# Last layer of a two-layer attention and feed-forward network: rows kept on the chip, weights quantised earlier, row scaling on ScalarE

## The chip, the cores and the metric

The kernel runs on one core of a Trainium2 chip. Its engines are TensorE (matrix products and transposes), VectorE, ScalarE, GpSimd, and SyncE, which issues all the DMAs that are spoken of here. Each runs its own list of instructions in order and waits for the others by semaphores. The metric is the device time of one execution in microseconds (us).

## What is computed

Two layers, each a cross attention and a feed-forward part, on x of 8 batches x 512 rows x 256 columns. The first layer has 16 heads of 64 and experts chosen per batch; the second has 16 heads of 16 and a quantised feed-forward part. Cut to the last layer:

```python
x = x + _L1_xattn_ref(_layernorm(x), ctx_768, ...)        # the second attention
x = x + _L1_ffn_ref(_layernorm(x), W_in, b_in, W_out, b_out)

def _L1_ffn_ref(x, W_in, b_in, W_out, b_out):             # 256 -> 1024 -> 256
    W_in_sim  = quantize_w8_per(W_in, axis=0)             # 127 / largest of a column
    W_out_sim = quantize_w8_per(W_out, axis=1)            # 127 / largest of a row
    x_sim = quantize_a16(x)                               # 32767 / largest of all of x
    hidden = gelu(x_sim @ W_in_sim + b_in)
    hidden_sim = quantize_a16(hidden)                     # 32767 / largest of all of hidden
    return hidden_sim @ W_out_sim + b_out
```

## The kernel before

`build` calls four parts one after the other: `first_attention`, `experts`, `second_attention` and `quantised_layer`. The last two matter here. Between parts, and between the stages of the last one, a block ends: all engines meet, and each starts the next block's list.

**The second attention** goes over 8 batches with 4 groups of heads each (groups 0 to 31; b is the batch, n the group in it, G = 4b + n). While group G is worked on, VectorE takes the row maxima for group G + 1 (`take_max`, L1766). In group 31, the last, there is no next group, so VectorE's `attend` does only `keep_o(30)` and `divide(30)` (L1781 to L1788), and the same for group 31 when that is done. TensorE turns the divided rows (L1604), projects them (L1624), and VectorE adds them to `x_sb` (L1838), which holds x for all 8 batches: 128 partitions x 32 tiles of 256. SyncE stores each batch of `x_sb` to `x_between` in DRAM (L1423). Ahead of the last store it loads W_in, turned (`winT`), into `spare`, a tile that served as scratch before (L1421).

**The last layer** has three stages.

First stage. SyncE waits for the stores and loads x again, into the first two tiles of `hid` (`xt`, L2024 and L2027), then the biases, and W_out into `spare` once the turned weights are out of it (L2033). VectorE quantises W_in (`quantise_weights`, L1918 to L1935): the largest of each row, four small steps, eight scalings of 256 columns, one subtraction over 2048 columns. TensorE turns the rounded W_in in two rounds (L2043), ScalarE keeps them (L2062). Then for each batch: VectorE takes the statistics (`row_statistics`, L67 to L76), GpSimd raises the variance to -1/2 (L2107), VectorE scales the four row tiles (`scale_rows`, L84) into `xn` and takes their maximum (L2082); TensorE turns `xn` (L2054) and ScalarE keeps it in `xnT` (L2065). VectorE's order is statistics of batch b + 1, scaling of b, maximum of b, in a loop over pairs of batches. `xn` has two buffers, the PSUM tile `ps_tr` one. Then `whole_amax` (L1974 to L1990) makes one maximum of all.

Second stage. VectorE rounds x and splits it into a high and a low part with ScalarE, TensorE makes the hidden rows (L2180), ScalarE applies Gelu into `hid` (L2195), VectorE takes its maxima (L2147). Between the first two batches and the others VectorE quantises W_out. Another `whole_amax` ends it.

Third stage. VectorE rounds the hidden rows two tiles at a time (L2264), ScalarE splits off the high part (L2310, L2322), VectorE the low part (L2272), TensorE projects (L2359, L2361), VectorE scales the sums and adds x (L2280), which SyncE has read back from `x_between`, and SyncE stores the result.

Of the kernel before, what the change touches and what calls it, by code (L numbers as in the profile page):

```python
# [1211 lines left out]
def second_attention(nc, x_sb, ident, ident_r, mhalf, d, ctx_parts, x_dram, spare, s_win, s_xs):  # L1212

    with ExitStack() as ctx:
# [152 lines left out]
        def _(sp):  # L1368
# [38 lines left out]
            def batch(b, left):  # L1407
# [343 lines left out]
        def _(dve):  # L1751
# [59 lines left out]

            def keep_v(b, t):
# [91 lines left out]
def quantised_layer(nc, ident, ones, mhalf, d, x_dram, out, spare, s_win, s_xs):  # L1904
# [5 lines left out]
    with ExitStack() as ctx:  # L1910
# [3 lines left out]
        def quantise_weights(dve, w, whole, top, s, inv, loaded, need, s_wq):  # L1914

            dve.wait_ge(loaded, need)
            nc.vector.tensor_reduce(top[:], w[:], AX.X, ALU.max, apply_absolute_value=True  # L1918
                                    ).then_inc(s_wq, 1)
            dve.wait_ge(s_wq, 1)  # L1920
            nc.vector.tensor_scalar(top[:], top[:], TINY, None, ALU.max).then_inc(s_wq, 1)
            dve.wait_ge(s_wq, 2)
            nc.vector.reciprocal(s[:], top[:]).then_inc(s_wq, 1)
            dve.wait_ge(s_wq, 3)
            nc.vector.tensor_scalar(s[:], s[:], 127.0, None, ALU.mult).then_inc(s_wq, 1)
            dve.wait_ge(s_wq, 4)
            nc.vector.reciprocal(inv[:], s[:]).then_inc(s_wq, 1)

            for t in range(FFT):
                nc.vector.tensor_scalar(w[:, t, :], w[:, t, :], s[:, t:t + 1], MAGIC,  # L1930
                                        ALU.mult, ALU.add).then_inc(s_wq, 1)
            flat = w[:].rearrange("p t k -> p (t k)")
            whole = whole[:].rearrange("p t k -> p (t k)")
            dve.wait_ge(s_wq, 13)
            nc.vector.tensor_scalar(whole, flat, MAGIC, None, ALU.subtract).then_inc(s_wq, 1)  # L1935

# [6 lines left out]
        hid = sb("hid", [P, FFT, B * NQ])  # L1943
        wout = sb("wout", [P, FFT, D], F32R)
        bin_ = sb("b_in", [P, FFT])
        bout = sb("b_out", [P, D])
        win_max = sb("win_max", [P, FFT])
        win_s = sb("win_s", [P, FFT])
        win_inv = sb("win_inv", [P, FFT])
        wout_max = sb("wout_max", [P, FFT])  # L1950
        wout_s = sb("wout_s", [P, FFT])
        wout_inv = sb("wout_inv", [P, FFT])
# [39 lines left out]
        with ExitStack() as ab:  # L1992
# [4 lines left out]
            with ExitStack() as a:  # L1997

                xt = hid[:, 0:2, :].rearrange("p a (t f) -> p (a t) f", f=D)
# [4 lines left out]
                rstd = sb("rstd", [P, 2, QT], to=a)  # L2004
                ps_tr = psum("tr", [P, DCH, NQ], to=a)
                ps_w = psum("w", [P, DCH, 512], to=a)
                s_wout = sem("wout_loaded")
                s_wq = sem("weights_steps")
                s_wt = sem("weights_transposed")
                s_wk = sem("weights_kept")  # L2010
                s_xl = [sem("x_loaded0"), sem("x_loaded1"), sem("x_loaded")]
                s_ln = sem("ln_steps")
                s_rstd = sem("rstd")
                s_xn = sem("xn_ready")
# [447 lines left out]
```

## Time and profile before

| | us |
|---|---|
| median of 3 runs (lowest, highest) | 3272.8 (3272.36, 3278.39) |
| the profiled execution, by its own time | 3275.32 |
| the span that its trace covers | 3273.5 |

| engine | busy us | share of the span |
|---|---|---|
| TensorE (PE) | 3103.7 | 95% |
| VectorE (DVE) | 2266.9 | 69% |
| ScalarE (ACT) | 1631.7 | 50% |
| GpSimd (POOL) | 1315.2 | 40% |

A row of the view in order of time has the start in us from the span's start, the length, the engine, the line, the operation, what is written and read with partitions and columns, and how many of them were merged; in brackets stands how long the engine had been idle before and what ended that. A row of DMA issues has the count, the size of one, and the median us from issue to landing. A row of waits has us in total, times, and the longest.

### The profile page before, as it was taken

The page shows a single profiled execution, that of the slowest core. Times are in us where ns is not written, and L with a number is a line of the kernel's source. Part 1 is how long each engine was busy: PE and PEld are TensorE (multiplying, and loading weights), DVE is VectorE, ACT ScalarE, POOL GpSimd, SP SyncE. Part 2 cuts the span into 40 slices and gives each one's busy share as a digit, 9 for nine tenths or more (in the row PEclk, how much of TensorE's full clock was granted, in tenths as well). Part 3 has the DMA queues.
Part 4 walks back from the last instruction along what each step waited for, and adds up shares of the span by engine and source line. Part 5 has one row for each costly group of instructions (what it writes and reads, how often), then busy time and mean ns, then how long its engine had stood idle before and what let it go on. Part 6 is the DMA issues. An engine that isn't in the chain of part 4 may idle for free. (4 is left out here: it accounts for less than half of the span.)

```text
span 3273.5 us, 40355 instructions
## 1 busy us (share of the span) xinstructions
PE 3103.7 (95%) x14204; PEld 1888.6 (58%) x14204; DVE 2266.9 (69%) x3673; ACT 1631.7 (50%) x1850; POOL 1315.2 (40%) x617
## 2 busy tenths in 40 slices
PE   6999999999999999999999879799999999999588
PEld 4556656556566565565565446455555555554368
DVE  5765775765766757757747434788888888887589
ACT  3453443443444434534534412376576666666288
POOL 1774774764766657757747722200000000000102
PEclk8999999999999999999999989799999999999698
DMA  8444543463453544444534232322323223322202
GB/s 232 113 112 125 129 128 101 116 162 83 116 145 90 122 126 116 112 118 119 122 106 111 65 123 64 83 50 65 68 49 72 65 49 71 69 49 56 72 13 90
DMA packets 182474, 317.40 MB, mean 97 GB/s; under 512 B 35080, under 2 KB 94288, under 8 KB 182288
## 3 DMA queue, kind: packets, MB, share of 16 engines
q1 hardware_dynamic: 182288, 315.00, 38.8%
q8 instruction: 107, 1.75, 0.2%
q14 instruction: 79, 0.65, 0.1%
HBM read 92.58 MB, written 29.36 MB: 37 GB/s over the span
## 5 line engine op out<-in xcount | busy, mean ns | idle before, releaser
L916 POOL TENSOR_TENSOR a_prob_sum<-a_prob_sum,a_prob 128x1024 f32<-128x1024 f32 x384 | 919.3, 2394 | 56.7 <-POOL a_prob_sum L916 2.2
L627 ACT ACTIVATE a_prob<-a_t 128x1024 f32<-128x1024 f32 x512 | 517.0, 1025 | 644.3 <-PE a_t L444 458.6
L774 DVE TENSOR_REDUCE a_mhalves<-a_m 128x1 f32<-128x512 f32 x1024 | 688.8, 680 | 105.8 <-PE a_m L408 98.3
L1669 ACT ACTIVATE a_prob<-a_t 128x1024 f32<-128x1024 f32 x512 | 497.6, 1025 | 183.9 <-PE a_t L1510 183.2
L1766 DVE TENSOR_REDUCE a_mhalves<-a_m 128x1 f32<-128x512 f32 x807 | 537.6, 685 | 61.2 <-PE a_m L1489 56.7
L451 PE MATMUL a_o<-a_prob,a_v_all 128*64 128x512 f32 x2048 | 493.7, 604 | 0.0
L408 PE MATMUL a_m<-a_kh_n,a_qz 128*128 128x512 f32 x1024 | 416.9, 419 | 7.7 <-DVE a_kl_n L768 3.4
L916 POOL TENSOR_TENSOR a_prob_sum<-a_prob 128x1024 f32<-128x1024 f32 x64 | 153.5, 2398 | 539.1 <-ACT a_prob L627 474.2
L1489 PE MATMUL a_m<-a_vh,a_qz 128*128 128x512 f32 x807 | 337.6, 438 | 9.7 <-DVE x_sb L1838 4.4
L436 PE MATMUL a_t<-a_q_hl,a_k_hh 128*128 128x512 f32 x1024 | 324.1, 398 | 0.3 <-ACT a_prob L627 0.3
L444 PE MATMUL a_t<-a_q_hm,a_k_lm 66*128 66x512 f32 x1024 | 321.3, 395 | 0.0
L1510 PE MATMUL a_t<-a_qs,a_vs 128*128 128x512 f32 x1024 | 319.0, 401 | 1.7 <-ACT a_qs L1688 0.9
L408 PEld LDWEIGHTS a_m<-a_kh_n,a_qz 128*128 128x128 f32 x1024 | 187.6, 188 | 201.8 <-issue 95.7
L1880 POOL TENSOR_TENSOR a_rstd<-a_veps,mhalf 128x4 f32<-128x4 f32 x8 | 8.2, 1021 | 718.5 <-DVE a_veps L76 718.5
L790 DVE RECIPROCAL a_recip<-a_x 128x128 f32<-128x128 f32 x256 | 239.4, 944 | 48.8 <-PE a_x L467 48.8
L1517 PE MATMUL a_o<-a_prob,a_v_all 128*18 128x512 f32 x2048 | 269.7, 598 | 0.4 <-ACT a_prob L1669 0.4
L1489 PEld LDWEIGHTS a_m<-a_vh,a_qz 128*128 128x128 f32 x807 | 152.5, 190 | 191.4 <-DVE a_mhalves L1766 127.5
L765 DVE TENSOR_TENSOR a_ql_n<-a_x,a_qz 64x512 fp32r<-64x512 f32 x128 | 88.2, 689 | 245.5 <-ACT a_qz L643 243.4
L451 PEld LDWEIGHTS a_o<-a_prob,a_v_all 128*64 128x64 f32 x2048 | 125.1, 136 | 223.8 <-issue 193.6
L1510 PEld LDWEIGHTS a_t<-a_qs,a_vs 128*128 128x128 f32 x1024 | 185.2, 189 | 57.9 <-ACT a_prob L1669 16.0
L444 PEld LDWEIGHTS a_t<-a_q_hm,a_k_lm 66*128 66x128 f32 x1024 | 193.5, 189 | 43.3
L436 PEld LDWEIGHTS a_t<-a_q_hl,a_k_hh 128*128 128x128 f32 x1024 | 188.5, 189 | 50.0 <-ACT a_prob L627 9.5
(274 smaller groups left out, 4181.5 us busy)
## 6 DMA issues: line engine op xcount, KB each, us to landing
a_k_hh<-a_kh_n SPq DMA_DIRECT2D x256, 256.0 KB, 4.3
a_k_lm<-a_kl_n SPq DMA_DIRECT2D x128, 256.0 KB, 4.8
a_q_hl<-a_qz SPq DMA_DIRECT2D x128, 128.0 KB, 2.3
a_q_hm<-a_qz SPq DMA_DIRECT2D x128, 128.0 KB, 2.4
a_q_hl<-a_ql_n SPq DMA_DIRECT2D x128, 128.0 KB, 2.3
a_vs<-a_vh SPq DMA_DIRECT2D x256, 64.0 KB, 2.3
a_wq<-wq_parts SPq DMA_DIRECT2D x63, 256.0 KB, 2.7
a_wk<-wk_parts SPq DMA_DIRECT2D x63, 256.0 KB, 2.9
```

The source lines that it names most:

```text
L408: pe.matmul(ps_m[:, n, :], qz[:, hd, qt * P:(qt + 1) * P], kh_n[:, n * 512:(n + 1) * 512], start=True, stop=True).then_inc(s_mx, 1)
L436: pe.matmul(ps_t[t % 2][:, hd, :], k_hh[:, u, hd, keys], q_hl[:, u, hd, :], start=True, stop=False)
L444: mm = pe.matmul(ps_t[t % 2][:, hd, :], k_lm[0:HD0 + 2, u, hd, keys], q_hm[0:HD0 + 2, u, hd, :], start=False, stop=True)
L451: mm = pe.matmul(ps_o[hd * HD0:(hd + 1) * HD0, :], v_all[:, t, (2 * pr.p + hd) * HD0:(2 * pr.p + hd + 1) * HD0], prob[:, t % RING, hd, :], ...
L627: nc.scalar.activation(prob[:, t % RING], ps_t[t % 2][:, :, :], ACT.Exp, scale=SCALE0).then_inc(s_exp, 1)
L774: nc.vector.tensor_reduce(mhalves[:, qt, hd, n:n + 1], ps_m[:, n, :], AX.X, ALU.max).then_inc(s_max, 1)
L916: nc.gpsimd.tensor_tensor(acc, prob[:, (t - 1) % RING] if t == 1 else acc, prob[:, t % RING], ALU.add).then_inc(s_acc, 1)
L1489: pe.matmul(out, qz[:, u, h, qt * P:(qt + 1) * P], vh[:, G // 2 % 2, k * 512:(k + 1) * 512], start=True, stop=True).then_inc(s_mx, 1)
L1510: mm = pe.matmul(ps_t[j][:, h, :], vs[:, u, 2 * j + h, keys], qs[:, u, 2 * j + h, :], start=True, stop=True)
L1517: mm = pe.matmul(ps_o[QD * h:QD * h + VW, :], v_all[:, t, GH * n + h, :], prob[:, t % RB, h, :], start=(t == 0), stop=(t == KT - 1))
L1669: nc.scalar.activation(prob[:, t % RB, 2 * j:2 * j + 2, :], ps_t[j][:, :, :], ACT.Exp, scale=SCALE1).then_inc(s_exp, 1)
L1766: nc.vector.tensor_reduce(mhalfs[:, u, qt, h, k:k + 1], bank, AX.X, ALU.max).then_inc(s_max, 1)
```

## The change

It touches what lies between the second attention and the second stage.

- **Weights.** A new class `LastWeights` holds W_out, a raw half of it, and the scales, from before the experts on. SyncE loads W_in into `spare` and the first half of W_out into the raw tile, waits until VectorE has rounded that half, and loads the second. VectorE quantises the first half of W_out, W_in, and the second half of W_out in group 31, after the division of group 30.
- **Rows.** `x_sb` stays for the whole kernel. The last layer's first stage reads it in place of `xt`; the eight loads go. `hid` has six tiles, and the hidden tiles 0 and 1 are written over `x_sb`.
- **Scaling.** VectorE makes `shift` = -mean x rstd (128x4), and ScalarE makes `xn` = x x rstd + shift, four activations for a batch. VectorE's order is statistics of b + 2, maximum of b, shift of b + 2. The loops of this stage are written out.

```diff
@@ second_attention, SyncE, last batch
-                    sp.dma_start(spare[:], d["winT"].rearrange("(t p) k -> p t k", p=P)).then_inc(s_win, 16)
+                    sp.dma_start(spare[:], d["winT"].rearrange("(t p) k -> p t k", p=P)).then_inc(last.s_win, 16)
+                    halves = d["wout2"].rearrange("(h t p) n -> h p t n", h=2, p=P)
+                    sp.dma_start(last.raw[:], halves[0]).then_inc(last.s_wout, 16)
+                    sp.wait_ge(last.s_woutq, 6 + FFT // 2)
+                    sp.dma_start(last.raw[:], halves[1]).then_inc(last.s_wout, 16)
@@ second_attention, VectorE, attend of group 31
                 elif n > 0:
                     keep_o(G - 1)
                     divide(G - 1, n - 1)
+                    dve.wait_ge(last.s_wout, 16)
+                    quantise_weights(nc, dve, last.raw[:], last.wout[:, 0:FFT // 2, :], last.wout_max, last.wout_s,
+                                     last.wout_inv, range(FFT // 2), last.s_woutq, 0)
+                    dve.wait_ge(last.s_win, 16)
+                    quantise_weights(nc, dve, spare[:], spare[:], last.win_max, last.win_s, last.win_inv,
+                                     range(FFT), last.s_winq, 0)
+                    dve.wait_ge(last.s_wout, 32)
+                    quantise_weights(nc, dve, last.raw[:], last.wout[:, FFT // 2:, :], last.wout_max, last.wout_s,
+                                     last.wout_inv, range(FFT // 2, FFT), last.s_woutq, 6 + FFT // 2)
@@ quantised_layer
-        hid = sb("hid", [P, FFT, B * NQ])
+        hid_first = x_sb[:].rearrange("p (a t) f -> p a (t f)", a=2)
+        hid_rest = sb("hid", [P, FFT - 2, B * NQ])
@@ first stage, SyncE
-                        for u in range(2):
-                            sp.dma_start(xt[:, u * QT:(u + 1) * QT], x_view[:, u * QT:(u + 1) * QT, :]
-                                         ).then_inc(s_xl[u], 16)
-                        for b in range(2, B):
-                            sp.dma_start(xt[:, b * QT:(b + 1) * QT], x_view[:, b * QT:(b + 1) * QT, :]
-                                         ).then_inc(s_xl[2], 16)
...
-                        sp.wait_ge(s_wt, 2)
-                        sp.dma_start(spare[:], d["wout2"].rearrange("(t p) n -> p t n", p=P)).then_inc(s_wout, 16)
@@ first stage, ScalarE
-                        with act.Fori(0, B) as b:
+                        def scale(b):
+                            act.wait_ge(s_shift, b + 1)
+                            if b >= 2:
+                                act.wait_ge(s_tr, b - 1)
+                                act.wait_ge(s_xm, b - 1)
+                            for qt in range(QT):
+                                nc.scalar.activation(xn[:, b % 2, qt, :], x_sb[:, b * QT + qt, :], ACT.Identity,
+                                                     bias=shift[:, b % 2, qt:qt + 1],
+                                                     scale=rstd[:, b % 2, qt:qt + 1]).then_inc(s_xn, 1)
+                        scale(0)
+                        for b in range(B):
+                            if b + 1 < B:
+                                scale(b + 1)
                             act.wait_ge(s_tr, b + 1)
-                            nc.scalar.copy(xnT[:, :, bass.ds(b * NQ, NQ)], ps_tr[:]).then_inc(s_xnT, 1)
+                            nc.scalar.copy(xnT[:, :, b * NQ:(b + 1) * NQ], ps_tr[:]).then_inc(s_xnT, 1)
@@ first stage, VectorE
+                        def shifts(b):
+                            dve.wait_ge(s_rstd, b + 1)
+                            nc.vector.scalar_tensor_tensor(shift[:, b % 2, :], mv[:, b % 2, :, 0], -1.0,
+                                                           rstd[:, b % 2, :], ALU.mult, ALU.mult
+                                                           ).then_inc(s_shift, 1)
...
-                        quantise_weights(dve, spare, spare, win_max, win_s, win_inv, s_win, 16, s_wq)
...
+                        statistics(0)
+                        statistics(1)
+                        shifts(0)
+                        shifts(1)
+                        for b in range(B):
+                            if b + 2 < B:
+                                statistics(b + 2)
+                            largest(b)
+                            if b + 2 < B:
+                                shifts(b + 2)
@@ second stage, VectorE
-                    quantise_weights(dve, spare, wout, wout_max, wout_s, wout_inv, s_mm, 1, s_wq2)
```

VectorE from the end of the second attention into the first stage, before: the division of groups 30 and 31 (`a_o_n`), the sums into `x_sb`, and the start of the quantising (`f_win_max` are the largest of W_in's rows).

```order
L1786 RECIPROCAL a_recip<-a_o_rows 128x16
L1788 TENSOR_TENSOR a_o_n<-a_o_rows,a_recip 128x256
L1781 STREAM_TRANSPOSE a_o_rows<-a_o 128x512
L1786 RECIPROCAL a_recip<-a_o_rows 128x16
L1788 TENSOR_TENSOR a_o_n<-a_o_rows,a_recip 128x256
L1838 TENSOR_TENSOR x_sb<-a_o,x_sb 128x256
L1838 TENSOR_TENSOR x_sb<-a_x,x_sb 128x256
L1838 TENSOR_TENSOR x_sb<-a_m,x_sb 128x256 x2
L1215 UNCONDITIONAL_BRANCH
L2067 UNCONDITIONAL_BRANCH
L1918 TENSOR_REDUCE f_win_max<-spare 128x8
```

VectorE at the same place of the changed kernel, from the division of group 30 (`a_o_n`, now L1836) on; `last_wout_raw` is the raw half of W_out.

```order
L1836 TENSOR_TENSOR a_o_n<-a_o_rows,a_recip 128x256
L1237 TENSOR_REDUCE last_wout_max<-last_wout_raw 128x4
L1239 TENSOR_SCALAR last_wout_max<-last_wout_max 128x4
L1241 RECIPROCAL last_wout_s<-last_wout_max 128x4
L1243 TENSOR_SCALAR last_wout_s<-last_wout_s 128x4
L1245 RECIPROCAL last_wout_inv<-last_wout_s 128x4
L1248 TENSOR_SCALAR last_wout_raw<-last_wout_raw,last_wout_s 128x256 x4
L1251 TENSOR_SCALAR last_wout<-last_wout_raw 128x1024
L1237 TENSOR_REDUCE last_win_max<-spare 128x8
```

What stood behind the sums now stands between the two divisions: W_in's remaining steps and the second half of W_out follow in the same form, and only then the transpose and division of group 31.

VectorE for one batch in the loop of the first stage, before (`f_mv` are mean and variance; the rows named ISA are waits).

```order
L67 BN_STATS f_stats<-f_hid 128x6
L70 ISA
L71 MEMSET f_veps 128x4
L73 BN_AGGR f_mv<-f_stats 128x2 x4
L75 REGISTER_ALU
L76 TENSOR_SCALAR f_veps<-f_mv 128x4
L84 TENSOR_SCALAR f_xn<-f_hid,f_mv,f_rstd 128x256 x4
L2082 REGISTER_ALU
L2082 TENSOR_REDUCE f_x_max<-f_xn 128x1
```

The same of the changed kernel.

```order
L67 BN_STATS f_stats<-x_sb 128x6 x4
L71 MEMSET f_veps 128x4
L73 BN_AGGR f_mv<-f_stats 128x2 x4
L76 TENSOR_SCALAR f_veps<-f_mv 128x4
L2123 TENSOR_REDUCE f_x_max<-f_xn 128x1
L2117 SCALAR_TENSOR_TENSOR f_shift<-f_mv,f_rstd 128x4
```

The four scalings are gone from VectorE, and a step that reads GpSimd's `f_rstd` of the batch just measured closes each batch. ScalarE had only the weights and the copies; now its list for the first stage begins so (L2088 keeps the weights):

```order
L2088 CAST f_win<-f_w 128x2x512 x2
L2097 ACTIVATE f_xn<-x_sb,f_shift,f_rstd 128x256 x8
L2106 COPY f_xnT<-f_tr 128x2x512
L2097 ACTIVATE f_xn<-x_sb,f_shift,f_rstd 128x256 x4
L2106 COPY f_xnT<-f_tr 128x2x512
```

The scalings stand behind both copies of the weights, and each copy of turned rows behind the scalings of the next batch.

## Rows read from the trace of the kernel before

**Rows 1.** Stretches: start:end, length, then PE, PEld, DVE, ACT, POOL, clock, DMA.
```profile
3053.00:3057.00 4.00, 0.00 (x0) 0.00 (x0) 3.86 (x9) 0.00 (x0) 0.00 (x0) 0.94 0.51 167
3066.00:3068.00 2.00, 0.62 (x3) 0.21 (x1) 0.00 (x0) 1.01 (x1) 0.00 (x0) 0.82 1.10 348
3070.00:3100.00 30.00, 11.86 (x49) 9.48 (x50) 28.54 (x95) 6.07 (x6) 6.97 (x6) 0.50 0.07 24
3110.00:3114.00 4.00, 4.00 (x10) 3.13 (x11) 2.78 (x3) 3.11 (x3) 0.00 (x0) 0.50 0.02 4
3114.00:3182.00 68.00, 58.71 (x249) 45.83 (x247) 58.19 (x92) 56.82 (x72) 0.00 (x0) 1.00 0.00 0
...
3192.00:3197.00 5.00, 3.63 (x17) 3.33 (x17) 5.00 (x6) 3.68 (x6) 1.36 (x1) 0.50 0.01 3
...
3199.00:3273.00 74.00, 63.16 (x478) 61.63 (x476) 70.08 (x114) 60.52 (x80) 20.04 (x6) 0.93 0.30 100
```

**Rows 2.** In order of time: VectorE quantises W_in.
```profile
3052.95 2.29 DVE L1918 TENSOR_REDUCE f_win_max<-spare 128x8 f32<-128x2048 f32 x1 [0.86 <-PEq L1215]
...
3056.04 2.14 DVE L1930 TENSOR_SCALAR spare<-spare,f_win_s 128x256 f32<-128x256 f32 x8
```

**Rows 3.** In order of time: TensorE and ScalarE, first stage; Gelus of the second.
```profile
3059.50 1.97 PE L2043 MATMUL f_w<-ident,spare 128*128 128x128 f32 x8 [7.87 <-DVE spare L1935]
...
3064.64 1.01 ACT L2062 CAST f_win<-f_w 128x1024 fp32r<-128x1024 f32 x1 [2.12 <-PE f_w L2043]
...
3098.80 1.01 ACT L2065 COPY f_xnT<-f_tr 128x1024 f32 x1 [3.56 <-PE f_tr L2054]
...
3099.95 1.94 PE L2054 MATMUL f_tr<-ident,f_xn 128*128 128x128 f32 x8 [1.28 <-ACT f_xnT L2065]
3102.02 1.01 ACT L2065 COPY f_xnT<-f_tr 128x1024 f32 x1 [2.21 <-PE f_tr L2054]
3103.34 0.16 DVE L1974 TENSOR_REDUCE f_amax_x<-f_x_max 128x1 f32<-128x8 f32 x1 [2.80 <-PEq L2018]
...
3131.94 4.94 ACT L2195 ACTIVATE f_hid<-f_h,f_b_in,f_h_scale 128x512 f32 x7
```

**Rows 4.** In order of time: statistics, GpSimd's power, scaling and maximum, first stage.
```profile
3059.36 1.40 DVE L67 BATCH_NORM_STATS2 f_stats<-f_hid 128x6 f32<-128x256 f32 x4
...
3061.21 0.17 DVE L76 TENSOR_SCALAR f_veps<-f_mv 128x4 f32<-128x4 f32 x1
...
3061.46 1.02 POOL L2107 TENSOR_TENSOR f_rstd<-f_veps,mhalf 128x4 f32<-128x4 f32 x1 [237.55 <-DVE f_veps L76]
...
3063.21 1.38 DVE L84 TENSOR_SCALAR f_xn<-f_hid,f_mv,f_rstd 128x256 f32<-128x256 f32 x4
3063.39 1.25 POOL L2107 TENSOR_TENSOR f_rstd<-f_veps,mhalf 128x4 f32<-128x4 f32 x1 [0.91 <-DVE f_veps L76]
...
3070.06 1.41 DVE L67 BATCH_NORM_STATS2 f_stats<-f_hid 128x6 f32 x4 [4.21 <-DMA f_hid<-x_between]
...
3092.21 1.22 DVE L2082 TENSOR_REDUCE f_x_max<-f_xn 128x1024 f32 x1
3093.34 1.40 DVE L67 BATCH_NORM_STATS2 f_stats<-f_hid 128x6 f32 x4
```

**Rows 5.** Waits in the second stage: who waited for whom.
```profile
DVE f_h_max L2147 <- ACT f_hid L2195: 7.7, 27, 1.4
```

**Rows 6.** In order of time: SyncE's load of W_in, and VectorE in group 31.
```profile
3013.78 0.58 SPq L1421 DMA_DIRECT2D spare<-in_winT  x1
...
3024.83 0.42 DVE L1788 TENSOR_TENSOR a_o_n<-a_o_rows,a_recip 128x256 f32<-128x256 f32 x1
...
3043.17 0.72 DVE L1781 STREAM_TRANSPOSE a_o_rows<-a_o 128x512 f32<-128x512 f32 x1 [17.92 <-PE a_o L1517]
```

**Rows 7.** DMA issues from 3000 us on: count, size of one, us to landing.
```profile
spare<-in_winT SPq DMA_DIRECT2D x1, 1024.0 KB, 5.6
spare<-in_wout SPq DMA_DIRECT2D x1, 1024.0 KB, 8.4
```

More of the change, by code:

```diff
@@ L1209, in _, with __init__, sb, sem @@
             two_batches(B // 2 - 1, True)
-def second_attention(nc, x_sb, ident, ident_r, mhalf, d, ctx_parts, x_dram, spare, s_win, s_xs):
+class LastWeights:
+    def __init__(self, nc, ctx):
+        def sb(name, shape, dt=F32):
+            return ctx.enter_context(nc.sbuf_tensor("last_" + name, shape, dt))
+        def sem(name):
+            return ctx.enter_context(nc.semaphore("last_" + name))
+        self.wout = sb("wout", [P, FFT, D], F32R)
+        self.raw = sb("wout_raw", [P, FFT // 2, D])
+        self.win_max, self.win_s, self.win_inv = (sb("win_" + k, [P, FFT]) for k in ("max", "s", "inv"))
+        self.wout_max, self.wout_s, self.wout_inv = (sb("wout_" + k, [P, FFT]) for k in ("max", "s", "inv"))
+        self.s_win = sem("win_loaded")
+        self.s_wout = sem("wout_half_loaded")
+        self.s_winq = sem("win_steps")
+        self.s_woutq = sem("wout_steps")
+def quantise_weights(nc, dve, w, whole, top, s, inv, tiles, done, before):
+    cols = slice(tiles[0], tiles[-1] + 1)
+    top, s, inv = top[:, cols], s[:, cols], inv[:, cols]
+    nc.vector.tensor_reduce(top, w, AX.X, ALU.max, apply_absolute_value=True).then_inc(done, 1)
+    dve.wait_ge(done, before + 1)
+    nc.vector.tensor_scalar(top, top, TINY, None, ALU.max).then_inc(done, 1)
+    dve.wait_ge(done, before + 2)
+    nc.vector.reciprocal(s, top).then_inc(done, 1)
+    dve.wait_ge(done, before + 3)
+    nc.vector.tensor_scalar(s, s, 127.0, None, ALU.mult).then_inc(done, 1)
+    dve.wait_ge(done, before + 4)
+    nc.vector.reciprocal(inv, s).then_inc(done, 1)
+    for t in range(len(tiles)):
+        nc.vector.tensor_scalar(w[:, t, :], w[:, t, :], s[:, t:t + 1], MAGIC,
+                                ALU.mult, ALU.add).then_inc(done, 1)
+    dve.wait_ge(done, before + 5 + len(tiles))
+    nc.vector.tensor_scalar(whole.rearrange("p t k -> p (t k)"), w.rearrange("p t k -> p (t k)"), MAGIC, None,
+                            ALU.subtract).then_inc(done, 1)
+def second_attention(nc, x_sb, ident, ident_r, mhalf, d, ctx_parts, x_dram, spare, last, s_xs):
     with ExitStack() as ctx:
@@ L1901, in _, with quantised_layer @@
                 add_bias(b)
-def quantised_layer(nc, ident, ones, mhalf, d, x_dram, out, spare, s_win, s_xs):
+def quantised_layer(nc, x_sb, ident, ones, mhalf, d, x_dram, out, spare, last, s_xs):
     x_view = x_dram.rearrange("(t p) f -> p t f", p=P)
@@ L1912, in sb @@
             return to.enter_context(nc.sbuf_tensor("f_" + name, shape, dt))
[L1914 to L1935, printed above, removed]
         def psum(name, shape, to=ctx):
@@ L2038, in _ @@
                         for r in range(2):
-                            pe.wait_ge(s_wq, 14)
+                            pe.wait_ge(last.s_winq, 6 + FFT)
                             pe.wait_ge(s_wk, r)
@@ L2073, in statistics @@
-                        def statistics(b, u):
-                            row_statistics(nc, dve, rows_of(b), stats[:, u], mv[:, u], veps[:, u, :], s_ln, 10 * b)
-                        def normalise(b, u):
-                            if not (isinstance(b, int) and b < 2):
-                                dve.wait_ge(s_tr, b - 1)
-                            scale_rows(nc, dve, rows_of(b), mv[:, u], rstd[:, u, :], xn[:, u], s_rstd, b + 1, s_xn)
+                        def statistics(b):
+                            u = b % 2
+                            row_statistics(nc, dve, [x_sb[:, b * QT + qt, :] for qt in range(QT)], stats[:, u], mv[:, u],
+                                           veps[:, u, :], s_ln, 10 * b)
@@ L2236, in tiles @@
         def tiles(b, first, n):
-            return hid[:, first:first + n, bass.ds(b * NQ, NQ)]
+            return hidden(first, n, bass.ds(b * NQ, NQ))
         with nc.Block() as block:
```

89 lines of the change are left out of this document (35 added, 54 removed).

## The prediction

> **What bounds the kernel now.** I read four views in this order: the stretches of the last layer [rows 1], the order in time of VectorE, ScalarE and TensorE around the seam between the second attention and the last layer, the DMA issues, and the rows that can price what is new. The last layer has three stages. In the first, x is read back, normalised and turned, and the weights are quantised: it runs from the end of the attention (VectorE starts at 3052.95) to the last copy of the turned rows at 3102.02 + 1.01 = 3103.03 [rows 2, 3]. Over its steady part VectorE is busy 28.54 of 30 us, TensorE 11.86, ScalarE 6.07 [rows 1]: VectorE sets the pace, at (3093.34 - 3070.06) / 5 = 4.66 us for a batch [rows 4]. In the second stage all three engines are near 58 of 68 us, and VectorE waits for ScalarE's Gelus [rows 1, 5]; in the third VectorE has 70.08 of 74 us [rows 1]. The change takes work from VectorE in the first stage, and the reader should see in [rows 2] what stands ahead of the first batch: 6.4 us of weight quantisation, and a wait of 4.21 us for the third batch's rows [rows 4].
>
> **The change part by part.**
>
> **1. Quantising moves into the last attention group.** VectorE has nothing there: it ends the division of group 30 at 3024.83 + 0.42 = 3025.25 and starts again only at 3043.17, 17.92 us idle [rows 6]. W_in whole took from 3052.95 to the first statistics at 3059.36, 6.4 us, of which the four small steps have 0.80 (3052.95 + 2.29 = 3055.24 to 3056.04) [rows 2, 4]. A half of W_out has half the columns in the long steps and the same small ones: (6.4 - 0.8) / 2 + 0.8 = 3.6; I take 3.8, as the ends of instructions weigh more in short ones. The three together: 3.8 + 6.4 + 3.8 = 14.0 us, so VectorE is free at 3039.3, 3.9 us before the output of group 31 asks for it. Cost nothing; beyond 3.9 us it costs one for one, because TensorE then waits for the divided rows. ScalarE and TensorE run that group by themselves and need nothing of VectorE in it. The loads: SyncE's queue issues W_in at 3013.78 [rows 6] and the first half right behind; 1024 KB landed in 5.6 us [rows 7], so both are there by about 3022. The second half is issued when the first is rounded, at 3029.1, and is wanted at 3035.5. Its price lies between 2.8 us, half of W_in's 5.6, and the 8.4 us of a 1024 KB load that stood behind the other reads [rows 7]; I take the former, since the queue is empty then, and even 8.4 would cost 2 of the 3.9 us. Behind that new wait SyncE has only the store of the last batch, not due before 3052. In the first stage the move takes away 6.4 us ahead of batch 0. W_out's 6.4 us in the second stage gain nothing: VectorE made them up, since it waited 27 times for a Gelu later, 7.7 us in all, and the stage goes by ScalarE [rows 5].
>
> **2. Rows stay in x_sb.** Eight loads and the 4.21 us wait go [rows 4]. The store of the last batch is still waited for, but only by SyncE for two bias loads: with at most 8.4 us for each of the two steps [rows 7] that is over 10 us before the stage ends. The hidden tiles 0 and 1 lie in the same memory later, at the same stride; nobody reads it then: nothing.
>
> **3. VectorE's work for a batch.** The four scalings (1.38 us as a group [rows 4]) leave; a 128x4 step for minus mean times rstd comes. Statistics take 3061.21 - 3059.36 = 1.85 us up to the start of the variance step. Then comes the maximum, 3093.34 - 3092.21 = 1.13 us, beside which GpSimd computes rstd: it starts 0.25 us behind the variance step and takes 1.02 to 1.25 us [rows 4]. The new step must wait for it, so it starts 1.35 to 1.6 us behind the variance step and not 1.2. With 0.17 us for itself the period is 1.85 + 1.4 + 0.17 = 3.4 to 3.6; I take 3.45, since what ran beside the 1.02 was statistics and beside the 1.25 a scaling, and a maximum is nearer to the first. The Trainium skill bears on this (GPSIMD Engine Reference, Specifications): GpSimd's SBUF interface is contended by VectorE's 2-port modes and by two SBUF inputs. A maximum is neither, so by it the period is the lower 3.4; the trace's 1.02 and 1.25 agree with it.
>
> **4. ScalarE's work for a batch.** Four activations with a bias and a scale per partition, 128x256. No row has that shape; the nearest is the Gelu with both operands on 512 columns, seven in 4.94 us, 0.70 apart [rows 3]. Half of its columns at most halve it: 0.35 to 0.70 each, 1.4 to 2.8 us for four. I take 0.5, near the lower end as the columns make most of such an instruction, so 2.0 for four. With its copy of 1.01 ScalarE has 3.0 of 3.45 us. The Trainium skill speaks against this move (ScalarE: Activation LUTs, Rules for kernel authors): multiply and add belong on VectorE, and by the formula for pointer operands in its section What ACT_TABLE_LOAD costs the four would take about 2.07 us (estimate), where VectorE's rows show 1.38. On this path the trace makes the slower engine free of charge, as it idles 24 of 30 us [rows 1].
>
> **5. The chain between TensorE and ScalarE.** A batch's transposes wait for the copy before them: 3098.80 + 1.01, then TensorE 3099.95 to 3101.89, the next copy at 3102.02. That is 3.22 us a batch at half clock [rows 3], as long as the four scalings (2.0) fit beside the transposes.
>
> **The sum.** VectorE starts at 3052.95 with statistics 0 and 1 (to 3056.8), GpSimd's rstd 1 is there at 3058.1, statistics 2 end at 3060.3. ScalarE first keeps the weights, now ready at once: two rounds took 3059.50 to 3064.64 + 1.01 = 6.15 us at half clock [rows 3], about 4.4 at full. The clock stood at 0.94 of full when the stage began [rows 1], at 0.50 later; TensorE no longer idles 7.87 us there, so I allow both. Scalings of batch 0 then end at 3061.1 or 3059.4, the step for batch 2 at 3062.6 or 3061.7, and that for batch 7 five periods later at 3079.9 or 3079.0. From the first copy, which ends at 3064.2 or 3062.6, the chain of point 5 needs seven more batches: 3064.2 + 22.5 = 3086.7. In the other case VectorE is last: scale 7 to 3081.0, copy 6 to 3082.0, transposes, copy 7 to 3085.3. The middle, 3086.0, is 17.0 us ahead of 3103.03. The maximum over all (3103.34) and both later stages follow as they are. So the profiled execution, 3275.3 us (its span 3273.5 and 1.8 around it), becomes 3258.3; it lies 2.5 us above the median of the runs, 3272.8, which becomes **3255.8**.
>
> **The rivals.**
> - **Full clock through the stage.** For it: after the weights' transposes and those of batch 0 in quick succession the clock was granted 0.82 for a while [rows 1], and the batches now follow each other more closely. Against it: from 3070 to 3100, with the same transposes once in 4.66 us, it was 0.50 throughout [rows 1]. The last transposes save 1.0 us more (end 3084.3), and the first ten matmuls of the second stage, 4.0 us at half clock [rows 1], would take 2.4 at the 58.71 / 249 = 0.24 us of later. Gain 18.7 + 1.6 = 20.3: 3252.5.
> - **A new wait on GpSimd in place of the work removed.** VectorE used a batch's rstd one batch later; now it stands waiting for it in every batch with nothing behind it that could go first. If GpSimd's answer costs 0.6 us more than rows show, or ScalarE's four activations take 2.8 us, so that 2.8 + 1.0 + 0.2 = 4.0 us is the period, five to seven periods are 3 to 4 us longer: 3259.5.
> - **The cover runs out.** Quantising in the group takes longer than 17.9 us (slower writes beside the exponentials, a late half). Speaks against it: maxima beside exponentials kept their length in the groups before. Each us beyond 3.9 of slack costs one; 4 us: 3259.8.
> - **Slower: the third stage at half clock.** It begins at 0.50, where 17 matmuls took 3.63 us, 0.213 each; a batch has 64, so 13.7 us. From 3199 on it ran at 0.93 and 478 matmuls took 74 us, 9.9 for 64, VectorE's pace [rows 1]. If the start, which moves, left TensorE at half clock, each further batch would cost 3.8 us and the change would lose from the fifth on; for seven 26.6: 3282.4. Nothing in the change touches that stage, and its row shows the clock rising by itself; little speaks for it.
>
> **How the numbers follow.** Forecast (15 to 18.5 us gained) 0.62; full clock 0.12; the wait or ScalarE's price 0.12; cover 0.06; half clock in the third stage 0.03; rest spread. A measurement of this kernel can tell about 0.2%, 6.5 us, from no change: faster needs a gain over that, so faster 0.92, same 0.05, slower 0.03. The range for 8 in 10 is 3251.5 (all of the full clock and a period of 3.4) to 3261 (period 4.0, plus a run's scatter).
>
> **What would show it.** In the changed profile: VectorE's quantising ends near 3039 and its next step shows an idle before it of about 4 us; the first statistics start near 3053; the starts of statistics lie 3.4 to 3.6 apart; four scalings on ScalarE take 2.0; the last copy of turned rows ends near 3086; from the maximum over all to the end (3103.34 to 3273.5 now [rows 3]) 170.2 us as before. Wrong if TensorE waits for the division after the last group, if the period is near 4, or if either later stage has another length.

## The result, and the profile after

The changed kernel takes **3254.52 us** (median of 4 runs, 3253.12 to 3256.76), the kernel before 3272.97 (4 runs, 3272.36 to 3278.39): ratio 0.9941, 95% interval 0.9923 to 0.9958, 18.5 us less. The profiled execution took 3254.05 us, its span 3252.2; that of before 3275.32 and 3273.5.

I cut both spans at four marks: the first matmul of the attention's first projection, VectorE's first step behind its last addition to x, the maximum over all rows (first stage ends), and the maximum over all hidden values (second stage ends). The last column is how long after the second stage's first matmul TensorE's clock rose, seen in its matmuls, which then took 0.39 us and no longer 0.63. Two more executions of the unaltered changed kernel stand beside it, from the runs e9 and e11 below; all in us.

| kernel | start | to the last layer | first stage | second | third | clock rises after |
|---|---|---|---|---|---|---|
| before | 64.1 | 2988.8 | 50.39 | 78.05 | 92.1 | 4.78 |
| after | 62.2 | 2988.7 | 31.60 | 76.85 | 92.9 | 3.15 |
| after, in e9 | 64.3 | 2987.9 | 31.80 | 77.32 | 92.3 | 4.00 |
| after, in e11 | 62.1 | 2988.4 | 31.66 | 76.88 | 92.9 | 3.12 |

So the first stage gave 18.6 to 18.8 us; the second 0.7 to 1.2; the third gave back 0.2 to 0.8; and the 2 us less at the start of the program are not the change's: in e9 the same kernel starts at 64.3, as late as before. By the three stages of the last layer alone, all three profiles of after are 19.1 to 19.2 us below before. The third stage's own work did not change: between its first roundings of hidden rows and its last low part VectorE takes 80.7 us in every trace. What it gave back are 0.2 us in the maximum over all hidden values (not in e9) and 0.5 us between VectorE's last step and the end (2.65 us in before, 3.18 in after); with the rows read back (e3) that end takes 2.64 again and in e2 2.97, so it moves between executions, and nothing ties it to the change.

First, VectorE in the last attention group, in order of time (start, length, engine, line, what it writes and reads; in brackets its idle time before and who ended it):

```profile
3021.75 0.72 DVE L1829 STREAM_TRANSPOSE a_o_rows<-a_o 128x512 f32<-128x512 f32 x1 [1.74 <-PE a_o L1565]
...
3022.79 0.43 DVE L1836 TENSOR_TENSOR a_o_n<-a_o_rows,a_recip 128x256 f32<-128x256 f32 x1
3023.13 1.21 DVE L1237 TENSOR_REDUCE last_wout_max<-last_wout_raw 128x4 f32<-128x1024 f32 x1
...
3026.85 2.28 DVE L1237 TENSOR_REDUCE last_win_max<-spare 128x8 f32<-128x2048 f32 x1
...
3033.25 1.21 DVE L1237 TENSOR_REDUCE last_wout_max<-last_wout_raw 128x4 f32<-128x1024 f32 x1
...
3036.36 0.69 DVE L1251 TENSOR_SCALAR last_wout<-last_wout_raw 128x1024 fp32r<-128x1024 f32 x1
3041.11 0.72 DVE L1829 STREAM_TRANSPOSE a_o_rows<-a_o 128x512 f32<-128x512 f32 x1 [4.06 <-PE a_o L1565]
```

The idle 17.92 us of [rows 6] hold the three quantisations (3.7, 6.4 and 3.8 us), no row of them waits for a load, and 4.06 us are left. Next, all engines at the start of the first stage:

```profile
3050.89 1.41 DVE L67 BATCH_NORM_STATS2 f_stats<-x_sb 128x6 f32<-128x256 f32 x4 [0.85 <-PEq L1258]
3051.05 1.06 PE L2071 MATMUL f_w<-ident,spare 128*128 128x128 f32 x8 [1.47 <-PEq L1258]
...
3053.30 1.06 PE L2071 MATMUL f_w<-ident,spare 128*128 128x128 f32 x8 [1.19 <-ACT f_win L2088]
...
3055.31 4.04 ACT L2097 ACTIVATE f_xn<-x_sb,f_shift,f_rstd 128x256 f32<-128x256 f32 x8
3055.97 0.16 DVE L2117 SCALAR_TENSOR_TENSOR f_shift<-f_mv,f_rstd 128x4 f32<-128x4 f32 x1 [1.06 <-POOL f_rstd L2145]
3056.05 1.40 DVE L67 BATCH_NORM_STATS2 f_stats<-x_sb 128x6 f32<-128x256 f32 x4
3057.44 1.42 PE L2080 MATMUL f_tr<-ident,f_xn 128*128 128x128 f32 x8 [3.07 <-ACT f_xn L2097]
...
3057.89 0.17 DVE L76 TENSOR_SCALAR f_veps<-f_mv 128x4 f32<-128x4 f32 x1
3057.97 1.21 DVE L2123 TENSOR_REDUCE f_x_max<-f_xn 128x1 f32<-128x1024 f32 x1
3058.14 1.01 POOL L2145 TENSOR_TENSOR f_rstd<-f_veps,mhalf 128x4 f32<-128x4 f32 x1 [2.21 <-DVE f_veps L76]
3059.18 0.17 DVE L2117 SCALAR_TENSOR_TENSOR f_shift<-f_mv,f_rstd 128x4 f32<-128x4 f32 x1
...
3059.26 1.40 DVE L67 BATCH_NORM_STATS2 f_stats<-x_sb 128x6 f32<-128x256 f32 x4
```

Where before had 6.4 us of quantising and a wait of 4.21 us for rows [rows 2, 4], TensorE turns the weights at once, eight in 1.06 us and not 1.97 [rows 3], and no VectorE step waits for a load. A batch of VectorE takes 3059.26 - 3056.05 = 3.21 us, where it took 4.66. The end of the stage, ScalarE and TensorE:

```profile
3078.03 1.01 ACT L2106 COPY f_xnT<-f_tr 128x1024 f32<-128x1024 f32 x1
3081.17 1.01 ACT L2106 COPY f_xnT<-f_tr 128x1024 f32<-128x1024 f32 x1 [2.12 <-PE f_tr L2080]
```
```profile
3079.19 1.94 PE L2080 MATMUL f_tr<-ident,f_xn 128*128 128x128 f32 x8 [1.19 <-ACT f_xnT L2106]
```

The last copies lie 3.14 us apart: a copy (1.01), the transposes behind it (1.94 at half clock), and the next copy at once. So the end of the stage goes by the chain of TensorE and ScalarE of [rows 3]. VectorE's batch is a little longer (3.21), but VectorE starts ahead of the chain and keeps most of that lead: no scaling waits for a shift. The stretches of the changed kernel (columns as in [rows 1]), the last one early in the third stage:

```profile
3053.00:3057.00 4.00, 1.06 (x8) 0.86 (x8) 2.86 (x15) 2.75 (x6) 2.02 (x2) 1.00 0.13 34
3057.00:3060.00 3.00, 1.42 (x8) 1.02 (x8) 2.92 (x13) 3.00 (x6) 1.01 (x1) 0.68 0.00 0
3060.00:3090.00 30.00, 15.54 (x61) 12.39 (x62) 21.48 (x73) 20.74 (x34) 5.03 (x5) 0.50 0.00 1
3090.00:3095.00 5.00, 5.00 (x19) 4.00 (x18) 3.09 (x4) 4.51 (x6) 0.00 (x0) 0.78 0.01 2
3095.00:3160.00 65.00, 56.13 (x239) 43.76 (x237) 52.23 (x76) 54.73 (x69) 0.00 (x0) 1.00 0.00 0
...
3162.00:3180.00 18.00, 11.36 (x59) 10.78 (x60) 17.00 (x20) 15.77 (x20) 5.55 (x2) 0.57 0.19 59
```

### The profile page after: what moved, and what is told of

Read it like the earlier page. It is cut to its first block and busy times, and to the rows that moved or that the text cites. A ratio compares the mean times of both kernels' runs of the same rounds, so it can differ in the third digit from the quotient of the medians.

```text
span 3252.2 us, 40235 instructions
## 1 busy us (share of the span) xinstructions
PE 3098.2 (95%) x14204; PEld 1885.1 (58%) x14204; DVE 2258.3 (69%) x3655; ACT 1646.5 (51%) x1882; POOL 1313.5 (40%) x617
```

## The experiments

Each starts from the changed kernel, with the time of one run unless a median is given. Stage lengths come from the traces, between the marks above; where the first stage begins with another step, its start is put 1.28 us behind the start of VectorE's last addition to x, as in the others. The time of a single run says little about edits of a few us: in these traces the start takes 62.1 to 66.8 us, and the way from there to the last layer 2985.3 to 2989.2 (e6 aside), whatever was edited behind it. So the stage lengths carry the comparison.

**e1: what is ScalarE's scaling worth?**

```diff
-nc.scalar.activation(xn[:, b % 2, qt, :], x_sb[...], ACT.Identity, bias=shift[...], scale=rstd[...])
+scale_rows(nc, dve, [x_sb[...] ...], mv[:, b % 2], rstd[:, b % 2, :], xn[:, b % 2], s_rstd, b + 1, s_xn)
```

> The changed kernel with the row scaling back on VectorE (ScalarE only copies; rows and weights stay as changed). The first stage, from VectorE's first statistics to the maximum over all, is 31.6 us in the changed kernel. Theory: VectorE sets the pace again with about 1.93 + 1.51 + 1.13 = 4.6 us a batch, 36.6 in all, and about 2.5 us of turning behind its last scaling: 39 us, so +7.4. Rival, that the chain of transposes and copies (3.13 us a batch) already sets the pace and the move to ScalarE gains nothing: 31.6 to 32.5.

Measured: 3264.92 us; first stage 38.64, 7.0 more than the changed kernel. VectorE's batch takes 4.49 us, and GpSimd's power beside the scaling 1.25 again:

```profile
3075.32 0.17 DVE L76 TENSOR_SCALAR f_veps<-f_mv 128x4 f32<-128x4 f32 x1
3075.41 1.38 DVE L84 TENSOR_SCALAR f_xn<-x_sb,f_mv,f_rstd 128x256 f32<-128x256 f32 x4
3075.57 1.25 POOL L2144 TENSOR_TENSOR f_rstd<-f_veps,mhalf 128x4 f32<-128x4 f32 x1 [3.23 <-DVE f_veps L76]
```

The move to the slower engine, 2.07 us for what VectorE did in 1.38, is worth 7.0 us.

**e2: is quantising W_out ahead worth anything?** W_out is loaded during the first stage, once the turned weights are out of `spare`, and quantised as one in the second.

```diff
-quantise_weights(nc, dve, last.raw[:], last.wout[:, 0:FFT // 2, :], ...)        # and the second half
+quantise_weights(nc, dve, spare[:], last.wout[:], ..., range(FFT), last.s_woutq, 0)   # behind low(1, 1)
```

> The changed kernel with W_out loaded in the first stage and quantised in the second, as before the change. The second stage, from one maximum over all to the next, took 78.05 us before and 76.85 after the change. Theory: VectorE's 6.4 us there are made up and the difference comes from TensorE's clock, so it stays near 76.9. Rival: the 1.2 us are W_out's, and it is 78.0 again. The first stage stays at 31.6 in both.

Measured: 3254.8 us; first stage 31.60, second 76.80. The 6.4 us of VectorE in the second stage cost nothing, and the second stage's shortening isn't theirs.

**e3: rows read back.** Eight loads x_between to x_sb behind the store, and a wait for each ahead of its statistics.

```diff
+sp.dma_start(x_sb[:, b * QT:(b + 1) * QT, :], x_view[:, b * QT:(b + 1) * QT, :]).then_inc(s_again[b], 16)
+dve.wait_ge(s_again[b], 16)
```

> The changed kernel with the rows of every batch loaded again from DRAM over the same tile before their statistics. Theory: the store must land (3.0 us) and the first 512 KB must come (about 2 to 3), so the first statistics start 5 to 6 us later; ScalarE's copies of the weights (to 3055.4) hide a part, and the later batches arrive faster than 3.1 us each: first stage 36 to 37 us, +4.5 to 5.5. Rival: loads stay ahead and only the 4.21 us seen before counted, hidden in part: +0 to 2.

Measured: 3260.43 us; first stage 37.42, 5.8 more, all of it ahead of batch 0:

```profile
3057.64 1.40 DVE L67 BATCH_NORM_STATS2 f_stats<-x_sb 128x6 f32<-128x256 f32 x4 [6.82 <-DMA x_sb<-x_between]
```

**e4: W_in quantised at the start of the first stage.**

```diff
-                    quantise_weights(nc, dve, spare[:], spare[:], last.win_max, ...)   # group 31
+                        quantise_weights(nc, dve, spare[:], spare[:], last.win_max, ...)
                         statistics(0)
```

> The changed kernel with W_in quantised at the start of the first stage, ahead of the statistics (W_out stays in the last group). Theory: ScalarE must keep the weights before it scales, so everything shifts by the 6.4 us of quantising, plus 1.7 us if TensorE's clock falls to half while it idles: first stage 38.0 to 39.8 us. Rival: statistics of two batches and the power hide a part: under 36.

Measured: 3264.32 us; first stage 39.97, 8.4 more, a little over the upper end. Above the 6.4 us of VectorE stand 2 us of TensorE, which idled and turned the weights at half clock:

```profile
3058.62 1.97 PE L2068 MATMUL f_w<-ident,spare 128*128 128x128 f32 x8 [7.86 <-DVE spare L1251]
```

**e5: is the chain of TensorE and ScalarE the bound?** A second PSUM buffer for the turned rows, so that transposes need not wait for the copy before them.

```diff
-ps_tr = psum("tr", [P, DCH, NQ], to=a)
+ps_tr = psum("tr", [P, 2, DCH, NQ], to=a)
-if b:
-    pe.wait_ge(s_xnT, b)
+if b >= 2:
+    pe.wait_ge(s_xnT, b - 1)
```

> The changed kernel with a second PSUM buffer for the turned rows, so that a batch's transposes no longer wait for the copy before. The copies stand 3.13 us apart in the changed kernel. Theory: the chain of TensorE and ScalarE has ScalarE's 2.07 + 1.01 less what they overlap in it, so only TensorE's part of the wait goes: copies 2.95 to 3.05 apart until VectorE's 3.22 us binds, then 3.2; the first stage 31.0 to 31.6 us. Rival: TensorE's half clock is what costs, and the stage shortens by 7 x (3.13 - 2.1) = 7 us to about 24.5.

Measured: 3253.01 us; first stage 30.07, 1.5 less and below what was expected; second stage 77.56, 0.7 more than in the profile of after, with the clock rising 4.43 us into it. ScalarE's copies are first 2.87 us apart (3062.47 to 3065.34), ScalarE's own pace, and from the scalings of the sixth batch on it waits for VectorE (3.22):

```profile
3062.47 1.00 ACT L2106 COPY f_xnT<-f_tr 128x1024 f32<-128x1024 f32 x1
3063.36 2.08 ACT L2097 ACTIVATE f_xn<-x_sb,f_shift,f_rstd 128x256 f32<-128x256 f32 x4
3065.34 1.00 ACT L2106 COPY f_xnT<-f_tr 128x1024 f32<-128x1024 f32 x1
...
3072.62 2.07 ACT L2097 ACTIVATE f_xn<-x_sb,f_shift,f_rstd 128x256 f32<-128x256 f32 x4 [0.26 <-DVE f_shift L2117]
...
3077.82 0.99 ACT L2106 COPY f_xnT<-f_tr 128x1024 f32<-128x1024 f32 x1
3079.97 1.01 ACT L2106 COPY f_xnT<-f_tr 128x1024 f32<-128x1024 f32 x1 [1.17 <-PE f_tr L2080]
```

Three paces are within 0.35 us of each other: VectorE 3.22, the chain 3.13, ScalarE 2.87. The first copy starts 8.37 us behind VectorE's start in both kernels; the seven others then take 20.4 us here and 21.9 in the changed kernel. One us of that 1.5 is the last batch alone: its copy stands 2.15 us behind the one before and not 3.14, since its transposes no longer waited for that copy.

**e6: is the cover really used up at 4 us?** Three maxima over W_in that nothing reads, added work in the last group.

```diff
 dve.wait_ge(last.s_win, 16)
+for k in range(3):
+    nc.vector.tensor_reduce(last.extra[:, k, :], spare[:], AX.X, ALU.max)
```

> The changed kernel with three more maxima over W_in (2.28 us each, results unused) on VectorE in the last group. Theory: VectorE has 4.06 us to spare there, so the last division starts 3 x 2.25 - 4.06 = 2.7 us later against TensorE's last product, one for one: TensorE waits, and the time from the division of group 30 to the start of the first stage grows from 28.1 to 30.8 us. Rival: the slack is smaller or larger than the idle shown, because the exponentials slow down beside VectorE: a growth over 3.5 or under 2.

Measured: 3259.26 us. The maxima took 6.66 us; the turned output of group 31 comes with no idle before it:

```profile
3024.56 0.72 DVE L1830 STREAM_TRANSPOSE a_o_rows<-a_o 128x512 f32<-128x512 f32 x1 [1.74 <-PE a_o L1566]
...
3029.66 6.66 DVE L1866 TENSOR_REDUCE last_extra<-spare 128x8 f32<-128x2048 f32 x3
...
3046.36 0.71 DVE L1830 STREAM_TRANSPOSE a_o_rows<-a_o 128x512 f32<-128x512 f32 x1
```

From one turned output to the next 21.80 us, where the changed kernel has 3041.11 - 3021.75 = 19.36: 2.44 more, that is 6.66 less the slack of 4.06, within 0.2. From the division of group 30 to the first stage it grows from 28.1 to 30.5 us, 30.8 expected. First stage 31.61. The time doesn't show this cleanly: of its 5.2 us over the profile of after, 4.6 are this program's start (66.8), and ahead of group 30's output the attention took 1.8 us less, as it also did in e8 without such work.

**e7: does TensorE's clock set the second stage's length?** 18 transposes that nothing reads, added work ahead of that stage.

```diff
+for k in range(18):
+    pe.transpose(ps_h[:, 3, (k % 4) * P:(k % 4 + 1) * P], ident[:], ident[:])
```

> The changed kernel with 18 transposes of the identity matrix (results unused) on TensorE while it would wait for the first rounded rows of the second stage. Theory: the second stage's first matmuls run at half clock because TensorE stood still before; kept busy it starts them at full and the second stage shrinks from 76.85 by about 1.0 to 1.6 us. Rival: the Gelus set the pace from the start (table load, then 0.7 us each), and under 0.4 us is gained.

Measured: 3253.59 us; second stage 75.66, 1.2 less, first 31.59. The 18 transposes took from 3086.86 to 3090.46, and the clock rose while they ran; the stage's first matmul starts at 3090.29, at full clock:

```profile
3090.00:3095.00 5.00, 5.00 (x25) 3.87 (x24) 3.07 (x5) 4.12 (x5) 0.00 (x0) 1.00 0.00 0
```

**e8 and e9: e5 and e7 together, beside the changed kernel.** No new edit in either.

> Two edits together that each moved one stage of the changed kernel: two PSUM buffers for the turned rows in the first stage, and 18 dummy transposes on TensorE (added work that nothing reads) between the first and the second stage. Theory (first stage set by VectorE's 3.22 us a batch once ScalarE's copies need not wait for each other; second stage's first 4 us set by TensorE's clock): first stage 30.0 to 30.2 us as with the two buffers alone, second stage 75.6 to 76.0 us; the time 2.2 to 3.2 us under that of the changed kernel, 3251.0 to 3252.5 us. Rival (the two buffers only moved the end of the first stage to where the clock is still half, so that the second stage hands back what the first one gained): second stage over 76.8 us in spite of the dummy transposes, and the time within 1.3 us of the changed kernel's.

> The changed kernel once more, unaltered, beside the version with both edits, for an interval of the difference. 3253 to 3257 us, 0.4 to 0.8% under the kernel before; first stage 31.6 us, second 76.8 us. If the 2 us at the program's start came with the change, its first matmul is again about 2 us earlier than in the kernel before; if it is scatter of the start, it may stand anywhere between.

Measured, five runs each on one chip: e8 3253.13 us (3249.78 to 3253.62; ratio to before 0.9936, 0.9923 to 0.9950), the changed kernel 3253.81 (3252.14 to 3255.54; 0.9938, 0.9925 to 0.9952). In e8's trace the first stage is 30.05 as expected, the second 76.40, above 76.0: the clock rose 1.42 us into the stage in spite of the transposes, which ran at half clock throughout:

```profile
3082.00 4.08 PE L2205 MATMUL f_h<-ident 128*128 128x128 f32 x18 [1.36 <-PEq L2150]
```

Their 4.08 us also put the stage's first matmul 6.81 us behind the maximum over all, 6.51 in the changed kernel. By the three stages e8 is 2.3 to 2.4 us below the three profiles of after; by the medians 0.7, which the ranges don't separate. The profiled run of e8 is its fastest, 3249.78, and most of its lead comes from the attention (2985.3 us to the last layer, 2987.9 to 2988.7 in the changed kernel) and not from these edits. The rival isn't refuted either: in e5 and in e8 the second stage came out 0.7 us longer than the same stage without the second buffer (77.56 against 76.85, 76.40 against 75.66), each time with a later rise of the clock, so about half of what the first stage gained may have been handed back; but the unaltered kernel alone varies by 0.5 us there. It stays open.

**e10 and e11: statistics ahead, beside the changed kernel.** If VectorE's statistics bind, the free 4.06 us of the last group and its gap before the additions to x can take three of eight. It contains e8's edits.

```diff
+last_statistics(nc, dve, last, x_sb, 0)      # behind the quantising
+last_statistics(nc, dve, last, x_sb, 1)
 ...
+last_shifts(nc, dve, last, 0)                # behind the division of group 31
+last_shifts(nc, dve, last, 1)
+last_statistics(nc, dve, last, x_sb, 2)
 ...
-for r in range(2):                           # ScalarE, first stage
+for r in range(2):
+    scale(r)
     act.wait_ge(s_wt, r + 1)
     nc.scalar.copy(win[:, :, r * 512:(r + 1) * 512], ps_w[:])
```

> The version with both edits, and besides: the statistics of the first two batches are taken in the last attention group, in the 4.07 us that VectorE still had free there, their shifts and the statistics of the third batch before the last additions to x (a gap of 2.83 us), and ScalarE scales the first batch while TensorE turns the first half of the weights. Theory (the first stage of the version with two buffers is set by VectorE's 3.22 us a batch, of which 1.93 are statistics, and behind that by ScalarE's 2.87): VectorE's work in the stage falls from 25.8 us and 3.85 ahead to 20, ScalarE becomes the bound with 2 x 1.0 + 8 x 2.87 = 25 us; from VectorE's last addition to x to the maximum over all 26 to 28 us (31.3 with two buffers alone, 32.9 in the changed kernel), so the time 5 to 7 us under the changed kernel's, 3247 to 3249.5 us. The last group itself is no longer: the idle of VectorE ahead of its last turned output falls from 4.07 us to about 0.2. Rival (the slack was not free: statistics there hold up the last group, as three extra maxima did): the group grows by 1 to 3 us and the gain is under 4 us.

> The changed kernel unaltered, once more, on the same chip as the version with the early statistics, to take the difference between the two. 3253 to 3257 us; first stage 31.6 to 31.8 us; second stage 76.8 to 77.4 us, longer the later TensorE's clock rises in it (76.85 where it rose 3.15 us behind the stage's first matmul, 77.32 where it rose 4.00 us behind).

Measured, five runs each on one chip: e10 **3250.05 us** (3244.33 to 3250.53; ratio to before 0.9921, 0.9908 to 0.9935), the changed kernel 3255.10 (3253.73 to 3256.84; 0.9942, 0.9929 to 0.9956): 5.0 us less, and no run of the one reaches into those of the other. That is the lower end of the 5 to 7 us expected, with the median above 3249.5. The free time is used to the end, and the first scalings begin with the stage:

```profile
3042.66 0.17 DVE L76 TENSOR_SCALAR last_veps<-last_mv 128x4 f32<-128x4 f32 x1
3043.04 0.72 DVE L1844 STREAM_TRANSPOSE a_o_rows<-a_o 128x512 f32<-128x512 f32 x1 [0.21 <-PE a_o L1580]
```
```profile
3052.75 2.08 ACT L2112 ACTIVATE f_xn<-x_sb,last_shift,last_rstd 128x256 f32<-128x256 f32 x4 [6.71 <-PEq L1273]
...
3059.18 1.01 ACT L2124 COPY f_xnT<-f_tr 128x1024 f32<-128x1024 f32 x1 [0.58 <-PE f_tr L2099]
...
3074.43 2.09 ACT L2112 ACTIVATE f_xn<-x_sb,last_shift,last_rstd 128x256 f32<-128x256 f32 x4
3076.41 1.01 ACT L2124 COPY f_xnT<-f_tr 128x1024 f32<-128x1024 f32 x1
3078.58 1.01 ACT L2124 COPY f_xnT<-f_tr 128x1024 f32<-128x1024 f32 x1 [1.16 <-PE f_tr L2099]
```

From the last addition to x (3051.49) to the maximum over all (3079.90) it takes 28.41 us, 32.88 in the changed kernel; 26 to 28 was expected. ScalarE is the bound now, at 2.87 us a batch; what was overlooked is that its first scaling can start only when the attention's block has ended, 1.26 us behind that addition, that it waits twice for transposes (0.58 and 1.16), and that 0.3 us follow its last copy. The 5.0 us are those of all the edits together: against e8, which has the other two, the way from the last addition to the maximum over all is 2.9 us shorter (28.41 against 31.3), and the ratios to before, 0.9921 and 0.9936, have overlapping intervals. What the early statistics are worth alone is shown by the stage and not by the time.

## Why the prediction was right, and where its terms were off

The forecast was 3255.8 us; 3254.5 was measured. By its own steps:

- **Step 1, quantising in the last group.** Right to the tenth: halves of 3.7 and 3.8 us, 4.06 us of slack where 3.9 was forecast, no wait for a load; the halves landed in 5.2 us (median of the two), nearer to W_in's 5.6 than to the 2.8 taken, and no step of VectorE waited for it. e6 shows that each us beyond costs one. That W_out gains nothing: e2. What the step left out is TensorE: by e4 W_in ahead is worth 8.4 us and not 6.4, since TensorE no longer idles 7.9 us before it turns the weights, at half clock then (1.97 us for eight) and at full now (1.06).
- **Step 2, rows kept.** The wait is gone. Alone it is worth 5.8 us (e3), and not 4.21, as nothing else covers the first load then. The three single prices, 7.0, 5.8 and 8.4, make 21.2, more than the 18.8 of all three. A likely reason is that a read-back partly hides behind VectorE's quantising, as it did before; no run took out two parts at once.
- **Step 3, VectorE's batch, is the term that was off most for each batch:** 3.21 to 3.22 us and not 3.45. The step that failed is the wait for GpSimd, which was put at 1.35 to 1.6 us behind the variance step: in a steady batch VectorE doesn't wait. The power is done at 3058.14 + 1.01 = 3059.15, the maximum at 3057.97 + 1.21 = 3059.18, and the shift follows at once, 1.29 us behind the variance step. GpSimd's power took 1.01 us beside a maximum in all six such batches, and 1.24 to 1.26 beside the scaling of e1. The rule of the Trainium skill (GPSIMD Engine Reference, Specifications), which names 2-port modes and two SBUF inputs as what contends, agrees with that for the maximum. The shift costs 0.08 and not 0.17: the next statistics start inside it.
- **Step 4, ScalarE's four activations.** 2.07 to 2.08 us, 2.0 forecast. The estimate by the Trainium skill (ScalarE: Activation LUTs, What ACT_TABLE_LOAD costs), 2.07, was the better one. The rule of the Trainium skill (ScalarE: Activation LUTs, Rules for kernel authors), multiply and add belong on VectorE, would have cost 7.0 us here (e1).
- **Step 5, the chain, and the sum.** The chain ended the stage, as in the half-clock case; it took 3.13 us a batch and not 3.22, 0.6 us over seven. The weights were turned at full clock, which the sum had left open: batch 0 was scaled 6.50 us behind VectorE's start, 6.45 forecast for full and 8.15 for half, and the first copy ended 9.36 behind it, 9.65 or 11.25 forecast. Taking the middle of the two cases cost the forecast 0.8 us, and the copy came 0.3 us ahead of even the full-clock one; with the chain's 0.6 that is nearly all of the difference between 17.0 us forecast and 18.8 measured. For weights at full clock the sum had VectorE last, not the chain; with VectorE's batch at 3.22 it was the chain.
- **The later stages "follow as they are".** They nearly did: 169.6 to 169.7 us from the maximum over all to the end in the three profiles, 170.2 forecast. But "either later stage has another length" was a sign of being wrong, and the second stage has one, by the clock. The second stage varies by 0.5 us between executions of the same kernel and more between the experiments, with the moment at which TensorE's clock rises: 76.8 to 76.9 where it rose after 3.1 us (four traces), 77.3 to 77.7 after 4.0 to 4.9 (four), 78.25 after 6.1 (e1), 75.7 when it was full from the start (e7). That is 0.4 to 0.55 us for each us at half clock. Before lies at 78.05 after 4.8, so most of the 1.2 us are the clock's (some 0.8; the other 0.3 to 0.4 I can't place), and none are W_out's (e2).
- **The rivals.** Full clock through the stage: it was at 0.50 from 3060 to the end of the stage. A new wait on GpSimd: not in a steady batch; the only one is the 1.06 us ahead of the second shift. The cover: 4 us were left. The third stage fell to 0.50 within 1.4 us and rose 18 us in, as before; 92.3 to 92.9 us against 92.1.

Some luck is in the 1.3 us between forecast and median. For the profiled execution the forecast was 3258.3 us, and 3254.05 came: 1.8 from the first stage, 1.2 from the second, 2.0 from a start that moves by itself, less 0.8 from the third. The 2.5 us taken off for the distance of before's profile from its median then covered most of it, since the profile of after lies 0.5 us below its own median and not above. The mechanism, VectorE's work gone and the chain of TensorE and ScalarE ending the stage, is what the traces and e1 to e5 show.

## What to carry to other kernels

When a stage is bound by one engine, price the neighbours' pace too, a batch of each beside the other (here 3.22, 3.13 and 2.87 us): that tells how far the first relief goes, and that a slower engine can do the work for nothing. Idle time of the bounding engine in the stage ahead, where its operands are long there, takes work at no cost, up to the slack; beyond it each us costs one (e6). What the moved work is worth is another matter and has to be read at its old place: W_in's 6.4 us gave 8.4, since TensorE had stood still and then turned the weights at half clock (e4), W_out's gave nothing (e2), and 5.8 us of statistics, with ScalarE's first scaling moved up too, gave 2.9, as ScalarE came next (e10 against e8). Single prices of edits at the same place need not add up: 21.2 us one by one, 18.8 together.

## What the runs showed of the hardware

The granted clock at the seam is not the same in every execution of the same program. The first half of the last group's output projections ran at half speed in the profile of after, and all of them at full in that of e9, the same kernel, which makes 9.78 or 8.09 us from the turned output to VectorE's first step in the last layer. In eleven of the thirteen traces, before included, these are 9.67 to 9.78 us and the clock over the projections 0.68 to 0.70; in e8 and e9 they are 8.1 us, with 1.00 (first row after, second e9):

```profile
3044.17 1.88 PE L1672 MATMUL a_o<-a_wo,a_prob 128*128 128x256 f32 x4 [1.10 <-ACT a_prob L1763]
```
```profile
3047.15 1.13 PE L1672 MATMUL a_o<-a_wo,a_prob 128*128 128x256 f32 x4 [1.10 <-ACT a_prob L1763]
```

That 1.7 us is as large as the effect of e5 or e7, so for edits of this size only stages compared by themselves tell something, or many runs. The dummy transposes do bring the clock up earlier, but not at a fixed moment: 0.0, 0.45 and 1.42 us into the second stage in e7, e10 and e8, with the same 18 of them, and never before 3.07 us in the ten traces without them.
